# Layernorm sums moved from VectorE to GpSimd, and the statistics of three groups moved into the group loop

## The chip, the cores and the metric

The kernel runs on one core of one Trainium2 chip. The metric is the device time of one execution, in microseconds (us); less is better. Engines are called by the profile's names: PE (TensorE matmuls), PEld (TensorE weight loads), DVE (VectorE), ACT (ScalarE), POOL (GpSimd) and SP (SyncE, here only DMA issue).

## What is computed

A gated cross-attention layer followed by a gated mixture-of-experts layer, for x of shape 32 x 128 x 128 (32 samples of 128 rows, 128 features), 16 heads and 8 experts:

```python
x = x + tanh(g_xattn[0]) * xattn(ctx, layernorm(x), b, seq_len)     # first half
x = x + tanh(g_ffn[0])   * ffn(layernorm(x), wi, bi, wo, bo, ...)   # second half

# ffn: logits = h @ gate_w.T + gate_b; scores = softmax(logits); the top 2 of 8 experts
# per expert e: inter = h @ wi.T + bi + (h @ lora_A[e].T) @ lora_B[e].T
#               out += gate_e * (relu(inter) @ wo.T + bo)
# layernorm: (x - mean) / sqrt(var + 1e-5)
```

## The kernel before, in words

The first half, attention, goes over 16 pairs of samples (`PAIRS`), in a software pipeline of steps `q`, each with two samples `i` and four chunks `c`. The second half goes over 8 groups of 4 samples (`GROUPS`, 512 rows each). All engines have their instruction order written out by hand, and meet only at semaphores; an engine executes its list in order, so that an instruction behind a waiting one waits too.

**Between the halves.** Steps `q` = 16 to 18 (19 on VectorE) finish the attention of the last pairs and already start groups 0 and 1. At `(q - PAIRS, i, c)` VectorE's list has small blocks for the second half. For each group g the second half first needs:

- `X <- X + attention`, one 128 x 512 sum in SBUF. For groups 0 to 2 GpSimd makes it (`residual`, L630), for groups 3 to 7 VectorE does (L1337, at the head of `stats2_of(g, 0)`). Both count in `s_xadd`.
- `stats2_of(g, k)`: the layernorm statistics, four `bn_stats` (L1344), four `bn_aggr` (L1349) and one `tensor_scalar` that adds epsilon (`veps2`, L1351).
- `rsqrt2(g)` (L635) and `normalise2(g)` (four instructions, L643), both on GpSimd.
- `transpose_x` (PE, L1068), `copy_xT` and `x_high` (ACT, L825, L831), `x_low` (GpSimd, L648).

Before, the statistics of groups 3 and 4 come at (1, 0, 3) and (1, 1, 1), of group 5 at (2, 0, 3), of group 6 at (2, 1, 1), and of group 7 in group 0 of the loop, between `sum_experts(0, 1)` and `sum_experts(0, 2)`. Other blocks there are `gates_...` (L1375 to L1423, the choice of the two experts, some twenty small instructions per group), `mask_u` (L1432, four instructions), `u_low` (L1446), and `add_attention(15)` (L1321, L1326), which waits for the last transpose of the attention output on PE (L1055).

**The loop over groups.** PE runs `first_expert(g, c)` (three matmuls of x_part, three of u_part, L1102), `second_expert(g, c)` (three matmuls, L1102), and at the end `out_weights(g)` (32 matmuls, L1137). ACT makes `h1` (L849) after each `first_expert`. VectorE makes `sum_experts(g, c)`, written `hsum` (L1440), after each `second_expert`. The chunks use three PSUM banks in turn, so `first_expert` of chunk number i waits for `s_hs >= i - 2`: `first_expert(g, 3)` cannot start before `sum_experts(g, 0)` has ended. `out_weights(g)` waits for all four sums of its group. VectorE's order in the end of group g is: `sum_experts(g, 3)`, `u_low(g + 1)`, the gates of group g + 2 up to `gates_pick(0)`, `finish(g)` (L1456, four instructions, waits for `out_weights(g)`), the rest of those gates, then in the next group `mask_u(g + 2)` and `sum_experts(g + 1, 0)`. GpSimd's order in a group is `x_low(g + 1)`, `make_base(g)` (L657, L661), `rsqrt2(g + 4)`, `normalise2(g + 4)`.

The functions that the change touches, with what calls them:

Of the kernel before, what the change touches and what calls it, by code (L numbers as in the profile page):

```python
# [18 lines left out]
ALU = mybir.AluOpType  # L19
# [20 lines left out]
def flamingo(nc, x, ctx, seq_len, g_xattn, g_ffn, b, wi, bi, wo, bo, lora_a, lora_b, gate_w, gate_b, out):  # L40
    B, S, D = x.shape
# [12 lines left out]
    GT = 4  # L54
    GROUPS = B // GT
# [7 lines left out]
    with es:  # L63
# [439 lines left out]
        def _(pool):  # L503
# [183 lines left out]
            for q in range(PAIRS + 3):  # L687
                if 0 <= q - 1 < PAIRS:
                    split_max(q - 1)
                if q == 1:  # L690
                    third_part(3)
                if q + 4 < PAIRS:
                    permute_k(q + 4)
                if q >= 2 and q % 2 == 0 and q // 2 + 3 < len(BATCHES):
                    power(q // 2 + 3)
                if q == 2:
                    place_v(0)
                if 2 <= q and 2 * q - 3 < B:
                    place_v(2 * q - 3)
                if q + 4 < PAIRS:  # L700
                    normalise(q + 4)
                if 2 <= q and 2 * q - 2 < B:
                    place_v(2 * q - 2)
                if q == PAIRS - 4:
                    residual(0)
                    residual(1)
                if 1 <= q and q + 3 < PAIRS:
                    third_part(q + 3)

                if q == PAIRS - 3:  # L710
                    rsqrt2(0)
                    normalise2(0)
                if q == PAIRS - 2:
                    weight_low(wiT, wi_part, 2)
                    rsqrt2(1)
                    residual(2)
                if q == PAIRS - 1:
                    normalise2(1)
                    weight_low(bT, b_part, 5)
                if q == PAIRS:  # L720
                    x_low(0)
                    rsqrt2(2)
                    normalise2(2)
                if q == PAIRS + 1:
                    rsqrt2(3)
                    normalise2(3)


            for g in range(GROUPS):
                if g + 1 < GROUPS:  # L730
                    x_low(g + 1)
                make_base(g)
                if g + 4 < GROUPS:
                    rsqrt2(g + 4)
                    normalise2(g + 4)
# [478 lines left out]
        def _(dve):  # L1214
# [117 lines left out]
            def stats2_of(g, k):  # L1332

                o = NST2 * g
                if k == 0 and g >= 3:
                    dve.wait_ge(s_norm, NNORM * 2 * (g + 1))
                    dve.tensor_tensor(X[:, GT * g:GT * (g + 1), :], X[:, GT * g:GT * (g + 1), :],  # L1337
                                      KV[:, GT * g:GT * (g + 1), 0:D], ALU.add).then_inc(s_xadd, 1)
                if k == 0:
                    dve.wait_ge(s_xadd, g + 1)  # L1340
                if k < 2:
                    for t in range(2 * k, 2 * k + 2):
                        n = GT * g + t
                        dve.bn_stats(stats2[:, n, :], X[:, n, :]).then_inc(s_stat2, 1)  # L1344
                else:
                    for t in range(GT):
                        n = GT * g + t
                        dve.wait_ge(s_stat2, o + t + 1)
                        dve.bn_aggr(mv2[:, n, :], stats2[:, n, :]).then_inc(s_stat2, 1)  # L1349
                    dve.wait_ge(s_stat2, o + 2 * GT)  # L1350
                    dve.tensor_scalar(veps2[:, GT * g:GT * (g + 1)], mv2[:, GT * g:GT * (g + 1), 1], EPS, None,  # L1351
                                      ALU.add).then_inc(s_stat2, 1)
# [108 lines left out]
            for q in range(PAIRS + 4):  # L1461
                for i in range(2):
                    m, n = 2 * q + i, 2 * q + i - LAG
                    for c in range(CH):
                        if 0 <= m < B:
                            row_max(m, c)
                        if (q, i, c) == (0, 0, 1):
                            first_rest(2)
                        if (i, c) == ((1, 1) if q == 0 else (0, 3)) and q + 3 < PAIRS:
                            first_rest(q + 3)  # L1470
                        if (i, c) in ((0, 0), (0, 1)) and 0 <= q - 4 < PAIRS and q != PAIRS + 1:
                            add_attention(q - 4, c)
                        later = 12 + c if q == 1 else 12 + 2 * q + c // 2
                        if q >= 1 and i == 1 and later < B and (q == 1 or c % 2 == 1):
                            stats_of(later)
                        if q >= 2 and q % 2 == 0 and (i, c) == (0, 0) and q // 2 + 3 < len(BATCHES):
                            for later in range(*BATCHES[q // 2 + 3]):
                                aggregate(later)
                            variances(q // 2 + 3)

                        for g in range(3):
                            if (q - g, i, c) in ((PAIRS - 4, 1, 1), (PAIRS - 4, 1, 3), (PAIRS - 3, 0, 3)):
                                stats2_of(g, c // 2 if i else 2)
                        at = (q - PAIRS, i, c)
                        if at == (0, 0, 3):
                            gates_shift(0)
                        if at == (0, 1, 1):
                            gates_score(0)
                            gates_top(0)
                        if at == (0, 1, 2):  # L1490
                            gates_pick(0)
                            gates_drop()
                            gates_top(1)
                        if at == (0, 1, 3):
                            add_attention(PAIRS - 3, 0)
                            add_attention(PAIRS - 3, 1)
                            gates_pick(1)
                            gates_end(0)
                        if at == (1, 0, 1):
                            mask_u(0)  # L1500
                        if at == (1, 0, 3):
                            for k in range(3):
                                stats2_of(3, k)
                        if at == (1, 1, 1):
                            for k in range(3):
                                stats2_of(4, k)
                        if at == (2, 0, 2):
                            u_low(0)
                            gates_shift(1)
                        if at == (2, 0, 3):  # L1510
                            for k in range(3):
                                stats2_of(5, k)
                        if at == (2, 1, 0):
                            gates_score(1)
                            gates_top(0)
                            gates_pick(0)
                            gates_drop()
                            gates_top(1)
                            gates_pick(1)
                            gates_end(1)  # L1520
                        if at == (2, 1, 1):
                            for k in range(3):
                                stats2_of(6, k)
                        if (q, i, c) == (PAIRS - 2, 0, 3):

                            dve.wait_ge(s_wr, 16 * 5)
                            dve.tensor_scalar(nbi_col[:, :], bi_col[:, :], -1.0, None, ALU.mult).then_inc(s_shift, 1)
                            dve.tensor_copy(bi_wide[:, :, :],
                                            bi_col[:, :, None].to_broadcast([128, FC, 128])).then_inc(s_shift, 1)
                        if (q, i, c) == (PAIRS - 1, 0, 0):  # L1530
                            dve.wait_ge(s_wT, 4)
                            dve.wait_ge(s_wTc, 6)
                            dve.scalar_tensor_tensor(out=shift[:, :], in0=bo_rows[:, :], scalar=2.0, in1=qk_t[:, 256:256 + D],
                                                     op0=ALU.mult, op1=ALU.add).then_inc(s_shift, 1)


            for g in range(GROUPS):
# [3 lines left out]
                if g == 0:  # L1541
                    mask_u(1)
                sum_experts(g, 1)
                if g == 0:
                    for k in range(3):
                        stats2_of(GROUPS - 1, k)
                sum_experts(g, 2)
                sum_experts(g, 3)
                if g + 1 < GROUPS:
# [8 lines left out]
                if g + 2 < GROUPS:  # L1558
                    gates_drop()
                    gates_top(1)  # L1560
                    gates_pick(1)
                    gates_end(g + 2)


# [22 lines left out]
```

## Time and profile before

| | |
|---|---|
| median of 3 executions | 279.3 us (278.44 to 279.52) |
| the profiled execution's own time | 278.2 us |
| its span in the trace | 276.4 us |
| granted PE clock | full speed throughout |

The profiled execution's time is 1.8 us over its span: what lies around the traced instructions. All rows come from this one execution. A timeline row gives start and length in us from the span's start, engine, line, operation, output and inputs, and how many instructions are merged in it; square brackets give the idle time of the engine before it and what ended that. Merged rows overlap their neighbours by some hundredths of a us, because instructions are pipelined.

### The profile page before, as it was taken

To read this page: it belongs to the slowest core of one execution; us is meant where nothing else is said; L and a number is where in the kernel's file an instruction comes from. 1 tells how busy PE (TensorE), PEld (TensorE's weight loads), DVE (VectorE), ACT (ScalarE), POOL (GpSimd) and SP (SyncE) were. 2 spreads that over 40 slices of the span, in tenths; PEclk is the share of its full clock that TensorE was granted. 3 is DMA by queue.
4 is the path that set the end of the run, shared out by engine and by line. 5 is a ranking of instruction groups with operands and counts; after the bars stand their busy time and mean duration, and the time that the engine had idled before them with its cause. 6 is when DMAs were issued, how large, how long until landed. Compare 5 with 4: busy or idle time off the path is not lost.

```text
span 276.4 us, 8038 instructions
## 1 busy us (share of the span) xinstructions
PE 245.5 (89%) x2966; PEld 184.3 (67%) x2966; DVE 214.0 (77%) x623; ACT 163.0 (59%) x319; POOL 158.5 (57%) x306
## 2 busy tenths in 40 slices
PE   0368979899998999989999979999999999999895
PEld 0135556566665566656567658888888989897865
DVE  4778786899999999997949999858585858585432
ACT  5778785889897989896877642333334242323220
POOL 6888676687877786686892447090919250505120
PEclk9999999999999999999999999999999999999999
DMA  4749997736776866640000000101010101001011
GB/s 110 202 124 209 208 222 181 206 83 196 178 215 160 215 160 162 149 71 6 8 6 2 4 0 0 39 2 38 0 40 0 42 0 30 10 7 31 2 38 38
DMA packets 48461, 23.46 MB, mean 85 GB/s; under 512 B 7680, under 2 KB 48296, under 8 KB 48424
## 3 DMA queue, kind: packets, MB, share of 16 engines
q1 hardware_dynamic: 47520, 22.77, 34.5%
q8 instruction: 24, 0.39, 0.6%
q10 hardware_dynamic: 904, 0.19, 0.4%
q14 instruction: 13, 0.11, 0.1%
HBM read 7.29 MB, written 2.10 MB: 34 GB/s over the span
## 4 chain that ended last, share of the span: by engine, by line
PE 57%; DVE 24%; POOL 5%; ACT 5%; issue 5%; DMA 2%; ACTq 1%; POOLq 0%
PE bank L1102 21%; DVE negmax L1313 11%; PE bank_max L1137 10%; PE bank L1012 7%; PE bank L1044 5%; PE bank L1079 2%; DVE rest L1264 2%; PE bank L1055 2%; PE bank L1095 2%; PE bank L1018 2%; DMA b_rows<-in_L_xattn_b_dram 2%; DVE hsum L1440 2%; ACT stack L760 2%; DVE KV L1326 1%; PE bank L1068 1%
## 5 line engine op out<-in xcount | busy, mean ns | idle before, releaser
L1313 DVE TENSOR_REDUCE negmax<-bank 128x4 f32<-128x512 f32 x128 | 83.3, 680 | 10.7 <-PE bank L1012 10.6
L809 ACT ACTIVATE probs<-bank 128x512 f32<-128x512 f32 x128 | 71.7, 602 | 15.0 <-PE bank L1018 13.9
L1012 PE MATMUL bank<-stack 64*128 64x128 bf16 x512 | 51.9, 235 | 9.6 <-DVE negmax L1313 6.0
L1012 PEld LDWEIGHTS bank<-stack 64*128 64x128 bf16 x512 | 31.7, 101 | 31.2 <-DVE negmax L1313 19.8
L1102 PE MATMUL bank<-u_part,b_part 128*128 128x512 f32 x192 | 52.0, 399 | 0.1
L849 ACT ACTIVATE h<-bank,bi_col 128x512 f32<-128x512 f32 x32 | 22.1, 690 | 49.4 <-PE bank L1102 49.4
L1018 PE MATMUL bank<-stack 64*128 64x128 bf16 x512 | 48.5, 223 | 0.3
L1440 DVE SCALAR_TENSOR_TENSOR hsum<-bank,nbi_col,h 128x512 f32<-128x512 f32 x32 | 23.9, 748 | 24.0 <-PE bank L1102 24.0
L648 POOL TENSOR_TENSOR x_part<-KV,x_part 128x512 fp32r<-128x512 f32 x8 | 10.4, 1301 | 55.8 <-ACT x_part L831 55.8
L1044 PE MATMUL bank<-probs,vpad 128*32 128x128 f32 x1024 | 42.1, 283 | 0.0
L1102 PEld LDWEIGHTS bank<-u_part,b_part 128*128 128x128 f32 x192 | 35.5, 189 | 8.3 <-ACT h L849 0.5
L1018 PEld LDWEIGHTS bank<-stack 64*128 64x128 bf16 x512 | 29.3, 96 | 3.3 <-ACT probs L809 2.2
L1044 PEld LDWEIGHTS bank<-probs,vpad 128*32 128x32 f32 x1024 | 24.5, 110 | 9.8 <-issue 6.4
L1102 PE MATMUL bank<-x_part,wi_part 128*128 128x512 f32 x96 | 28.9, 409 | 1.8 <-DVE hsum L1440 1.8
L1137 PE MATMUL bank_max<-woT,hsum 128*128 128x128 f32 x232 | 28.0, 279 | 2.1 <-DVE hsum L1440 2.1
L1137 PEld LDWEIGHTS bank_max<-woT,hsum 128*128 128x128 f32 x232 | 26.5, 192 | 3.8 <-DVE hsum L1440 3.2
L603 POOL TENSOR_TENSOR part<-rest,part 128x512 bf16<-128x512 f32 x14 | 16.2, 1159 | 20.5 <-ACT part L802 20.5
L643 POOL TENSOR_SCALAR KV<-X,mv,rstd 128x128 f32<-128x128 f32 x32 | 25.6, 810 | 0.8
L1102 PEld LDWEIGHTS bank<-x_part,wi_part 128*128 128x128 f32 x96 | 16.9, 189 | 5.5 <-DVE hsum L1440 2.3
L815 ACT ACTIVATE o_rows<-bank 128x256 f32<-128x256 f32 x32 | 12.4, 388 | 7.5 <-PE bank L1044 7.5
L842 ACT ACTIVATE u_part<-bank 128x512 fp32r<-128x512 f32 x15 | 8.2, 595 | 11.5 <-PE bank L1102 11.5
L968 PE MATMUL bank<-ident,kperm 128*128 128x128 f32 x32 | 8.6, 361 | 6.8 <-ACT kperm L781 6.8
(136 smaller groups left out, 407.0 us busy)
## 6 DMA issues: line engine op xcount, KB each, us to landing
stack<-part SPq DMA_DIRECT2D x96, 128.0 KB, 3.0
KV<-in_ctx_dram SPq DMA_DIRECT2D x5, 512.0 KB, 4.1
X<-in_x_dram SPq DMA_DIRECT2D x7, 256.0 KB, 4.3
out_dram<-res SPq DMA_DIRECT2D x7, 256.0 KB, 2.3
KV<-in_ctx_dram SPq DMA_DIRECT2D x5, 256.0 KB, 5.6
stack<-bias_line SPq DMA_DIRECT2D x7, 48.0 KB
stack<-max_rows SPq DMA_DIRECT2D x13, 24.0 KB
X<-in_x_dram SPq DMA_DIRECT2D x2, 128.0 KB, 2.4
```

The source lines that it names most:

```text
L603: pool.tensor_tensor(pair_part(2, p), halves(rest[:, p % 2, :]), pair_part(1, p), ALU.subtract).then_inc(s_t3, 1)
L643: pool.tensor_scalar(spare(g)[:, t, :], X[:, n, :], mv2[:, n, 0:1], rstd2[:, n:n + 1], ALU.subtract, ALU.mult).then_inc(s_xh2, 1)
L809: act.activation(probs[:, i % 4, :], sc2[i % 2][:, :], ACT.Exp).then_inc(s_exp, 1)
L815: act.activation(o_rows[:, n % 4, :], o_acc[:, 256 * (n % 2):256 * (n % 2) + 256], ACT.Copy).then_inc(s_oc, 1)
L849: act.activation(h1[:, c, :], chunk_bank(i)[:, :], ACT.Relu, bias=bi_col[:, c:c + 1]).then_inc(s_h1, 1)
L1012: mm = pe.matmul(sc1[i % 2][:, j * 128:(j + 1) * 128], stack[at, s, h0 + 2 * j, q0:q0 + 128], stack[at, s, h0 + 2 * j, 512 + q0:640 + q0], ...
L1018: mm = pe.matmul(sc2[k % 2][:, j * 128:(j + 1) * 128], stack[at, t, h0 + 2 * j, 512 + q0:640 + q0], stack[at, t, h0 + 2 * j, q0:q0 + 128], ...
L1044: mm = pe.matmul(o_acc[32 * j:32 * j + 32, c0:c0 + 128], v_window(n, UNITS2[c], j), probs[:, i % 4, j * 128:(j + 1) * 128], start=(c % 2 = ...
L1102: mm = pe.matmul(dst, w[a], v[b], start=(start and k == 0), stop=(closed or (stop and k == 2)), skip_group_check=closed)
L1137: mm = pe.matmul(out_bank(g, t)[:, t * 128:(t + 1) * 128], hsum[:, c, t * 128:(t + 1) * 128], woT[:, c, :], start=(c == 0), stop=(c == FC ...
L1313: dve.tensor_reduce(negmax[:, p % 2, n % 2, 8 * (u // 2) + u % 2:8 * (u // 2) + u % 2 + 7:2], bank_cols(sc1[i % 2]), AX.X, ALU.max, negate ...
L1440: dve.scalar_tensor_tensor(out=hsum[:, c, :], in0=chunk_bank(i)[:, :], scalar=nbi_col[:, c:c + 1], in1=h1[:, c, :], op0=ALU.max, op1=ALU.a ...
```

## The change

GpSimd makes the sums of groups 3 to 7 too: `residual(3)` after `x_low(0)`, `residual(4)` at the next step, and `residual(g + 5)` in groups 0 to 2 of the loop, after `make_base(g)`. VectorE loses the sum from `stats2_of`. The statistics of group 4 move from (1, 1, 1) to (2, 0, 3), where those of group 5 stood; those of groups 5, 6 and 7 move to the end of groups 0, 1 and 2 of the loop, behind `gates_end(g + 2)`.

```diff
@@ gpsimd, the steps between the halves
                 if q == PAIRS:
                     x_low(0)
+                    residual(3)
                     rsqrt2(2)
                     normalise2(2)
                 if q == PAIRS + 1:
+                    residual(4)
                     rsqrt2(3)
                     normalise2(3)
@@ gpsimd, the loop over groups
                     x_low(g + 1)
                 make_base(g)
+                if g + 5 < GROUPS:
+                    residual(g + 5)
                 if g + 4 < GROUPS:
@@ vector, stats2_of(g, k)
-                if k == 0 and g >= 3:
-                    dve.wait_ge(s_norm, NNORM * 2 * (g + 1))
-                    dve.tensor_tensor(X[:, GT * g:GT * (g + 1), :], X[:, GT * g:GT * (g + 1), :],
-                                      KV[:, GT * g:GT * (g + 1), 0:D], ALU.add).then_inc(s_xadd, 1)
                 if k == 0:
                     dve.wait_ge(s_xadd, g + 1)
@@ vector, the steps between the halves
                         if at == (1, 0, 3):
                             for k in range(3):
                                 stats2_of(3, k)
-                        if at == (1, 1, 1):
-                            for k in range(3):
-                                stats2_of(4, k)
...
                         if at == (2, 0, 3):
                             for k in range(3):
-                                stats2_of(5, k)
+                                stats2_of(4, k)
...
-                        if at == (2, 1, 1):
-                            for k in range(3):
-                                stats2_of(6, k)
@@ vector, the loop over groups
                 sum_experts(g, 1)
-                if g == 0:
-                    for k in range(3):
-                        stats2_of(GROUPS - 1, k)
                 sum_experts(g, 2)
...
                     gates_end(g + 2)
+                if g + 5 < GROUPS:
+                    for k in range(3):
+                        stats2_of(g + 5, k)
```

## Rows read from the trace of the kernel before

**Rows 1.** The page, part 1: busy time, share of the span, instructions.

```profile
PE 245.5 (89%) x2966; PEld 184.3 (67%) x2966; DVE 214.0 (77%) x623; ACT 163.0 (59%) x319; POOL 158.5 (57%) x306
```


**Rows 2.** Busy us by stretch: stretch, length, PE, PEld, DVE, ACT, POOL; then granted clock.

```profile
152.70:170.64 17.94, 15.49 (x142) 11.60 (x141) 17.06 (x66) 8.73 (x18) 10.55 (x12) 1.00 0.00 1
...
188.82:203.20 14.38, 14.38 (x89) 12.56 (x89) 10.19 (x35) 5.09 (x9) 7.71 (x8) 1.00 0.07 19
```


**Rows 3.** The chain of waits in order of time: start us, length us, piece.

```profile
152.75 0.37 DVE rsum L1321
...
170.64 3.84 PE bank_max L1137 x32
```


**Rows 4.** Timeline of PE, 159 to 189 us: start us, length us, operation.

```profile
159.92 0.38 PE L1055 MATMUL bank<-ident,o_rows 128*128 128x128 f32 x2
...
161.28 0.86 PE L1102 MATMUL bank<-x_part,wi_part 128*128 128x512 f32 x3
...
165.35 0.97 PE L1102 MATMUL bank<-x_part,wi_part 128*128 128x512 f32 x3 [1.83 <-DVE hsum L1440]
166.16 1.54 PE L1102 MATMUL bank<-u_part,b_part 128*128 128x512 f32 x6
...
178.23 0.87 PE L1102 MATMUL bank<-x_part,wi_part 128*128 128x512 f32 x3
...
180.31 0.85 PE L1102 MATMUL bank<-x_part,wi_part 128*128 128x512 f32 x3
181.00 1.56 PE L1102 MATMUL bank<-u_part,b_part 128*128 128x512 f32 x6
...
184.98 3.84 PE L1137 MATMUL bank_max<-woT,hsum 128*128 128x128 f32 x32
```


**Rows 5.** Timeline of DVE from 143 us: start us, length us, operation.

```profile
144.65 0.33 DVE L1411 SCALAR_TENSOR_TENSOR score<-hot,score 128x32 f32<-128x32 f32 x1
...
155.35 0.68 DVE L1337 TENSOR_TENSOR X<-X,KV 128x512 f32<-128x512 f32 x1
156.07 0.87 DVE L1344 BATCH_NORM_STATS2 stats<-X 128x6 f32<-128x128 f32 x4
...
157.34 0.18 DVE L1386 TENSOR_REDUCE lsum<-lexp 128x4 f32<-128x32 f32 x1
...
160.77 0.68 DVE L1337 TENSOR_TENSOR X<-X,KV 128x512 f32<-128x512 f32 x1
...
162.67 1.19 DVE L1351 TENSOR_SCALAR veps<-mv 128x4 f32<-128x4 f32 x1
163.78 0.34 DVE L1321 RECIPROCAL rsum<-bank 128x32 f32<-128x32 f32 x1
...
167.19 0.69 DVE L1337 TENSOR_TENSOR X<-X,KV 128x512 f32<-128x512 f32 x1
...
169.18 1.41 DVE L1440 SCALAR_TENSOR_TENSOR hsum<-bank,nbi_col,h 128x512 f32<-128x512 f32 x2
...
177.41 0.76 DVE L1432 TENSOR_TENSOR u<-bank,hot 128x256 f32<-128x256 f32 x2
...
178.74 0.74 DVE L1440 SCALAR_TENSOR_TENSOR hsum<-bank,nbi_col,h 128x512 f32<-128x512 f32 x1
```


**Rows 6.** Instructions of line L1351: engine, operation, count, ns least/median/most.

```profile
L1351 DVE TENSOR_SCALAR veps<-mv x8: 170/174/1189, 118.2 to 169.1; 128x4 f32<-128x4 f32 x8
```


**Rows 7.** Timeline of POOL, 139 to 180 us: start us, length us, operation.

```profile
142.09 3.19 POOL L643 TENSOR_SCALAR KV<-X,mv,rstd 128x128 f32<-128x128 f32 x4
...
150.72 1.39 POOL L635 TENSOR_TENSOR rstd<-veps,half_neg 128x4 f32<-128x4 f32 x1 [5.03 <-DVE veps L1351]
...
162.55 1.29 POOL L648 TENSOR_TENSOR x_part<-KV,x_part 128x512 fp32r<-128x512 f32 x1 [7.20 <-ACT x_part L831]
...
179.03 1.30 POOL L648 TENSOR_TENSOR x_part<-KV,x_part 128x512 fp32r<-128x512 f32 x1 [8.15 <-ACT x_part L831]
```


**Rows 8.** Instructions of line L630: engine, operation, count, ns least/median/most.

```profile
L630 POOL TENSOR_TENSOR X<-X,KV x3: 1266/1282/1286, 110.0 to 127.6; 128x512 f32<-128x512 f32 x3
```


## The prediction

> **What bounds the kernel now.** I read the page first. PE is busy for 89% of the span, VectorE for 77% [rows 1]. Those are averages over two halves, so the second view is the busy time by stretch. In a group of the loop PE is busy for all 14.38 of 14.38 us and VectorE for 10.19 [rows 2]: the loop runs at PE's pace. From 152.70 to 170.64 us, where the attention runs out and group 0 begins, it is the other way round: VectorE 17.06 of 17.94 us, PE 15.49 [rows 2]. The third view, the chain of waits, says the same in another way: from 152.75 us it lies on VectorE, and goes back to PE only with `out_weights(0)` at 170.64 us [rows 3]. So VectorE's list sets the time in these 18 us, and what it costs is seen on PE's own timeline: `first_expert(0, 3)` starts at 165.35 us after PE idled 1.83 us for `hsum` [rows 4], and `out_weights(0)` starts late as well.
>
> How much can come back is read by setting group 0 against group 1, which has the same PE list. From the start of `first_expert(g, 2)` to the end of `out_weights(g)` group 1 takes (184.98 + 3.84) - 178.23 = 10.59 us [rows 4]. Group 0 takes from 161.28 [rows 4] to 170.64 + 3.84 = 174.48 us [rows 3], 13.20 us. The difference, 2.61 us, is all that VectorE costs PE here. 1.99 us of it is the wait ahead of `first_expert(0, 3)` (165.35 - 161.28 against 180.31 - 178.23 [rows 4]), and 0.62 us is the rest, mainly the wait ahead of `out_weights(0)`.
>
> **What the change removes between the halves.** Ahead of 152.75 us the statistics of group 4 and the sum of group 3 go; VectorE was free for the attention's last pairs there when PE's transpose came, so this alone gives nothing. After 152.75 us three things go from the list [rows 5]. At (2, 0, 3) statistics of group 4 without a sum stand for those of group 5 with one: 156.07 - 155.35 = 0.72 us less. At (2, 1, 1) all of group 6 goes: 163.78 - 160.77 = 3.01 us. In group 0 all of group 7 goes: 169.18 - 167.19 = 1.99 us. Together 5.72 us of VectorE's chain, more than twice what PE can take back.
>
> Is the first wait then gone in full? `hsum(0, 0)` released PE at 165.35 us [rows 4]. Without 0.72 + 3.01 us VectorE's list would reach that point at 161.6 us; it then waits for other things, `add_attention(15)` for the transpose of 159.92 + 0.38 us [rows 4] and `hsum` for `second_expert(0, 0)`, which ends where `first_expert(0, 2)` starts, 161.28 us. So it ends near 161.3 + 0.74 [rows 5] plus a hand-over, 162.2 us at most, and PE needs it at 161.28 + 2.08 = 163.36 us. More than 1 us is to spare. `mask_u(1)` follows (1.33 us, 178.74 - 177.41 [rows 5]) and ends before the transposes that need it. From there the sums follow PE as in group 1. I take the whole 2.61 us; the lower bound is 2.0 us, if only the first wait goes.
>
> **What it adds on GpSimd.** One `residual` takes 1.28 us [rows 8]. `residual(3)` and `rsqrt2(2)`, `normalise2(2)` behind it run in a stretch where GpSimd then idles: `rsqrt2(3)` waits 5.03 us, until 150.72 us, for VectorE's statistics [rows 7]. Two sums are 2.56 us, half of that. The new waits of `stats2_of(3)` and `stats2_of(4)` on VectorE for GpSimd are therefore met: `residual(3)` is done at about 142.3 us, and the statistics stand at about 148.6; `residual(4)` comes behind `normalise2(2)` and the last copies of v, at about 148.3 us, and is wanted at 155.35 us. If it were late, the gates of group 1 and all else in VectorE's list would stand behind it; the cover is 7 us. In the loop GpSimd is busy 7.71 of 14.38 us [rows 2] and idles 8.15 us ahead of `x_low` of a group [rows 7]. A `residual` more makes it 9.0 us. What is late next is `normalise2(g + 4)` by 1.28 us, which PE wants more than a group later. Cost nothing.
>
> **What it adds on VectorE in the loop.** The statistics without the sum take 157.34 - 156.07 = 1.27 us [rows 5]. They stand behind `gates_end` and ahead of `mask_u(g + 2)` and `hsum(g + 1, 0)`, and for the latter PE's `first_expert(g + 1, 3)` waits. On average VectorE has 4 us to spare per group, but not here. `hsum(1, 0)` ended at 178.74 + 0.74 = 179.48 us [rows 5], and `first_expert(1, 3)` started at 180.31 us [rows 4]: 0.83 us of cover. Part of the 1.27 us takes the place of a short hand-over ahead of `mask_u`; I take 1.15 to 1.27, so 1.2 us. With 0.05 us from a sum's end to PE's start (169.18 + 1.41 = 170.59 us [rows 5] and 170.64 [rows 3]), PE is late by 1.2 + 0.05 - 0.83 = 0.42 us. A late start also costs a little more, because the weight load is no longer under the matmul ahead: three x_part matmuls took 166.16 - 165.35 = 0.81 us behind the wait and 181.00 - 180.31 = 0.69 us without [rows 4], 0.12 us more. So 0.54 us a group. PE is full in these groups [rows 2], so nothing takes it back, and `finish(g)` of the next group moves with PE: the stall comes in groups 1, 2 and 3. Bounds for one: 0.37 us (1.15, no load) and 0.66 us (1.27, the load, 0.05 for a stretched gate). Three are 1.6 us, 1.1 to 2.0.
>
> The gates' small instructions may be stretched where `normalise2` now lies under them for 1.28 us more. At 142.09 to 145.28 us the two already overlap [rows 7], and the worst gate instruction took 0.33 us [rows 5]. I take 0.05 us a group for it, inside the bounds above. In the Trainium skill, "SBUF — State Buffer", section "Who interferes with whom", a VectorE instruction with two SBUF inputs contends with a GpSimd one that reads SBUF, and the later of the two blocks fully. By row the cost is the 0.05 us a group; by that rule it is a rival, below. This trace does not show such a full block for the gates.
>
> **Sum.** -2.6 + 1.6 = -1.0 us. The profiled execution's 278.2 us would be 277.2; it lay 1.1 us under the median of 279.3, which would be 278.3 us, 0.4% less. The bounds are -1.5 (2.6 and 1.1) and 0.0 (2.0 and 2.0), so 277.8 to 279.3 us. A change of 0.5%, 1.4 us, is about what a measurement of this kernel can tell from none.
>
> **Rivals.** *The statistics in the loop are hidden.* If VectorE's place behind `gates_end` had room for them, only the gain would be left: 279.3 - 2.6 = 276.7 us. For it speaks the spare 4 us per group; against it the 0.83 us at the one place. Chance 0.14.
>
> *The epsilon instruction meets `x_low` (slower).* `veps2` normally takes 0.17 us, but once 1.19 [rows 6]: at 162.67 us, just after `x_low` had started on GpSimd at 162.55 us, and it ended as that did [rows 5, 7]. In the loop the new one comes about 1.1 us behind the place where `mask_u` stood, 177.41 us, so at 178.5, and `x_low` starts at 179.03 us [rows 7]: it is ahead by 0.5 us. The point from which it decides: if VectorE is later by more than 0.5 us, it waits to 179.03 + 1.30 = 180.33 us, `mask_u` and `hsum` end at 182.40, and PE stalls 2.26 us a group in place of 0.54. Three groups: 279.3 - 2.6 + 6.8 = 283.5 us. Chance 0.07. The same section of the Trainium skill says that `tensor_scalar` in a two-port mode and GpSimd exclude each other for a whole instruction; by that rule, the trace agrees (1.19 against 0.17 us).
>
> *The gates are blocked by `normalise2`.* Each of its four instructions takes 3.19 / 4 = 0.80 us [rows 7], and the shift of 1.28 us puts at most two more under the gates. If these blocked a gate instruction in full, `finish` would be late by up to 1.6 us less the small slack; at one block a group, 0.8 us, the sum is 278.3 + 2.4 = 280.7 us. Against it stands the 0.33 us. Chance 0.08.
>
> *PE does not get its time back in group 0,* because behind VectorE something else is late, such as ScalarE's part of group 0 or the hand-overs. Then 0 to 1.6 us of gain stand against 1.6 us of stalls: 279.3 to 280.9 us. For it speaks that so many lists meet here; against it the 1 us to spare. Chance 0.13. My forecast has 0.58.
>
> **How the numbers follow.** Predicted is 278.3 us. The range leaves out the collision, most of the blocked gates and the top of the last case: 276.6 to 280.4 us; the likeliest case's own is 277.8 to 279.3. Faster by over 0.5% (under 277.9 us) are the hidden statistics and a quarter of the forecast's: 0.30. Slower by over 0.5% (over 280.7) are the collision, half of the blocked gates, some of the last case and a little for the measurement: 0.16. The rest is 0.54.
>
> **What would show it.** In the changed profile: PE without idle time ahead of `first_expert(0, 3)` and `out_weights(0)`, the latter ending 13.20 - 2.61 = 10.6 us behind the start of `first_expert(0, 2)`; L1337 gone and L630 eight times; PE idle (or its weight load) released by `hsum` once in each of groups 1, 2 and 3, by about half a us, so that these groups take 14.9 us and group 4 14.4 us; `veps2` always near 0.17 us. The prediction is wrong if a group with statistics takes 14.4 us or over 15.5 us, or if group 0 keeps a wait.

## The result, and the profile after

| | before | changed |
|---|---|---|
| median of 20 executions | 278.38 us | 276.29 us |
| the profiled execution's span | 276.4 us | 274.0 us |

The ratio is 0.9931, with a 95% interval of 0.9912 to 0.9949: 1.9 us less, 1.4 to 2.4. It leaves out disturbed executions, such as one of 1162.61 us of the kernel before. The forecast was 1.0 us less, 278.3 us, in a range of 276.6 to 280.4. The changed kernel is 2.0 us under the forecast time and 0.3 us under the range.

The first view of the changed kernel is the busy time by stretch: stretch, its length, then the busy us of PE, PEld, DVE, ACT and POOL with the number of instructions, and the granted clock. The stretches are the end of group 0 (from the start of `first_expert(0, 2)`) and groups 1 to 4, each up to the end of its `out_weights`.

```profile
160.26:170.83 10.57, 10.57 (x71) 9.49 (x70) 7.63 (x21) 3.89 (x8) 8.96 (x9) 1.00 0.00 0
170.83:185.64 14.81, 14.63 (x90) 12.49 (x89) 11.32 (x45) 5.08 (x9) 8.97 (x9) 1.00 0.07 19
185.64:200.43 14.79, 14.62 (x89) 12.48 (x89) 11.22 (x44) 5.08 (x9) 8.96 (x9) 1.00 0.07 19
200.43:215.23 14.80, 14.58 (x89) 12.47 (x89) 11.20 (x44) 5.08 (x9) 7.73 (x8) 1.00 0.06 18
215.23:229.57 14.34, 14.34 (x89) 12.56 (x89) 10.16 (x35) 5.08 (x9) 3.61 (x3) 1.00 0.07 20
```

The end of group 0 takes 10.57 us where it took 13.20 [rows 3, 4]: 2.63 us less, and PE is never idle in it. Groups 1, 2 and 3 take 14.81, 14.79 and 14.80 us where a group took 14.38 [rows 2]; group 4, with no statistics at its head, takes 14.34. The timeline of PE (start, length, operation, idle time before and its releaser) shows where:

```profile
160.26 0.86 PE L1106 MATMUL bank<-x_part,wi_part 128*128 128x512 f32 x3
...
162.34 0.87 PE L1106 MATMUL bank<-x_part,wi_part 128*128 128x512 f32 x3
...
166.99 3.84 PE L1141 MATMUL bank_max<-woT,hsum 128*128 128x128 f32 x32
...
174.60 0.85 PE L1106 MATMUL bank<-x_part,wi_part 128*128 128x512 f32 x3
...
177.03 0.95 PE L1106 MATMUL bank<-x_part,wi_part 128*128 128x512 f32 x3 [0.18 <-DVE hsum L1440]
...
181.80 3.84 PE L1141 MATMUL bank_max<-woT,hsum 128*128 128x128 f32 x32
```

`first_expert(0, 3)` follows at 162.34 us with no wait and `out_weights(0)` at 166.99 us with none. In the kernel before PE idled 1.83 us ahead of the first [rows 4] and 0.43 us ahead of the second:

```profile
170.64 3.84 PE L1137 MATMUL bank_max<-woT,hsum 128*128 128x128 f32 x32 [0.43 <-DVE hsum L1440]
```

In group 1 `first_expert(1, 3)` starts 177.03 - 174.60 = 2.43 us behind `first_expert(1, 2)` where it was 2.08 [rows 4]: it now waits for `hsum(1, 0)`. The timeline of DVE shows what stands ahead of that sum, `bn_stats` from 173.64 us, the epsilon instruction (`bn_aggr` lies between them) and `mask_u(2)`:

```profile
145.59 1.43 DVE L1417 TENSOR_TENSOR lsum<-top 128x4 f32<-128x4 f32 x1
...
160.46 0.75 DVE L1440 SCALAR_TENSOR_TENSOR hsum<-bank,nbi_col,h 128x512 f32<-128x512 f32 x1 [0.27 <-PE bank L1106]
...
173.64 0.86 DVE L1344 BATCH_NORM_STATS2 stats<-X 128x6 f32<-128x128 f32 x4
...
174.82 0.17 DVE L1351 TENSOR_SCALAR veps<-mv 128x4 f32<-128x4 f32 x1
174.90 0.76 DVE L1432 TENSOR_TENSOR u<-bank,hot 128x256 f32<-128x256 f32 x2
...
176.23 1.40 DVE L1440 SCALAR_TENSOR_TENSOR hsum<-bank,nbi_col,h 128x512 f32<-128x512 f32 x2
```

and the timeline of POOL has the sums, and `x_low` of groups 0, 1 and 2:

```profile
138.62 1.27 POOL L648 TENSOR_TENSOR x_part<-KV,x_part 128x512 fp32r<-128x512 f32 x1
139.85 1.27 POOL L630 TENSOR_TENSOR X<-X,KV 128x512 f32<-128x512 f32 x1
...
145.74 1.27 POOL L630 TENSOR_TENSOR X<-X,KV 128x512 f32<-128x512 f32 x1
...
161.53 1.30 POOL L648 TENSOR_TENSOR x_part<-KV,x_part 128x512 fp32r<-128x512 f32 x1 [7.08 <-ACT x_part L835]
...
165.16 1.28 POOL L630 TENSOR_TENSOR X<-X,KV 128x512 f32<-128x512 f32 x1
...
175.40 1.31 POOL L648 TENSOR_TENSOR x_part<-KV,x_part 128x512 fp32r<-128x512 f32 x1 [4.72 <-ACT x_part L835]
```

The epsilon instruction starts at 174.82 us, takes 0.17 us and has ended 0.4 us before `x_low(2)` starts at 175.40 us. One line was not foreseen: at 145.59 us DVE needs 1.43 us for an addition of 128 x 4 numbers (L1417) that otherwise takes 0.15 us. It ends at 147.02 us, as `residual(4)` does, whose start is recorded at 145.74 us.

From `first_expert(0, 2)` to the end of the span 276.4 - 161.28 = 115.12 us in the trace before [rows 4] became 274.0 - 160.26 = 113.74 us, 1.4 us less. The other 1.0 us of the spans' difference was there already when `first_expert(0, 2)` began, and at `x_low(0)`, 138.62 us here, 139.70 before: ahead of the first instruction that the change touches.

### The profile page after: what moved, and what is told of

Its sections match the earlier page's. It is cut to its first block, busy times and chain, and to the rows that moved or that the text cites. A ratio compares the mean times of both kernels' runs of the same rounds, so it can differ in the third digit from the quotient of the medians.

```text
span 274.0 us, 8038 instructions
## 1 busy us (share of the span) xinstructions
PE 245.4 (90%) x2966; PEld 184.0 (67%) x2966; DVE 211.0 (77%) x618; ACT 163.0 (59%) x319; POOL 163.7 (60%) x311
## 4 chain that ended last, share of the span: by engine, by line
PE 54%; DVE 26%; ACT 5%; POOL 5%; issue 5%; DMA 2%; ACTq 1%; POOLq 0%; DVEq 0%
PE bank L1106 19%; DVE negmax L1317 12%; PE bank_max L1141 9%; PE bank L1016 6%; PE bank L1048 6%; DVE rest L1268 3%; PE bank L1083 3%; PE bank L1099 2%; PE bank L1059 2%; PE bank L1022 2%; DMA b_rows<-in_L_xattn_b_dram 2%; DVE hsum L1440 2%; DVE u L1432 2%; ACT stack L764 2%; ACT probs L813 1%
```

## The experiments

Each median is that of the kernel's own executions; a ratio is against the kernel before on the same chip.

### Sums to GpSimd alone, in one row

```diff
@@ gpsimd: residual(3) after x_low(0), as in the changed kernel
                 if q == PAIRS + 1:
+                    residual(4)
+                    residual(5)
+                    residual(6)
                     rsqrt2(3)
                     normalise2(3)
+                    residual(7)
@@ stats2_of: no sum on VectorE; all statistics stay where they were before
```

> The five sums go to GpSimd, the statistics of groups 3 to 7 stay where they were in the kernel before. My theory (VectorE's list bounds the kernel only from 152.7 to 170.6 us, PE can take back 2.6 us there, and statistics at the ends of groups 0 to 2 cost a stall of 0.4 us each): VectorE loses three sums of 0.72 us ahead of hsum(0, 3), and its epsilon instruction of group 6 no longer meets x_low(1), so another 1.0 us; hsum(0, 0) ends about 2.4 us earlier, in time for PE. The full 2.6 us come back and no stall is paid: 2.6 us under the kernel before, about 1.2 us under the changed one. Rival (the move of the statistics is what brings the gain): only 1.4 us under the kernel before, slower than the changed one.

The median of its 6 executions is 280.87 us, beside 278.59 for the kernel before; 2.6 us less were expected, so this is a miss. No ratio is given: five of the six had a granted clock under 1, down to 0.976, and the one at full clock took 276.70 us, where the kernel before at full clock has a median of 278.0. The times alone thus do not say how this kernel compares; the trace says what went wrong in it. The first two fences are its timelines of DVE and POOL, the third that of PE.

```profile
146.34 3.89 DVE L1418 TENSOR_TENSOR lsum<-top 128x4 f32<-128x4 f32 x1
```

```profile
146.49 3.72 POOL L630 TENSOR_TENSOR X<-X,KV 128x512 f32<-128x512 f32 x3
```

```profile
151.44 0.66 PE L1100 MATMUL bank<-ident,u 128*128 128x128 f32 x4 [2.21 <-DVE u L1433]
...
153.69 2.06 PE L1084 MATMUL bank<-agT,KV 128*128 128x136 f32 x8
```

L1418 here is L1417 of the other kernels. VectorE's addition of 128 x 4 numbers, two inputs in SBUF, stands for 3.89 us and ends at 150.23, as the third of three GpSimd sums in a row does (146.49 + 3.72 = 150.21 us). `mask_u(0)` is late, PE idles 2.21 us for it, and eight matmuls that take 1.19 us in the changed kernel take 2.06 us behind the gap, where the granted clock is 0.76 from 150 to 154 us and 0.81 from 154 to 158. From `x_low(0)` to `first_expert(0, 2)` it is 165.00 - 139.38 = 25.62 us, 4.0 us more than the 21.64 of the changed kernel. So GpSimd's sums can hold VectorE, and PE's idle time has a second price. Behind that the trace has what the theory said, 171.74 + 3.84 - 165.00 = 10.58 us for the end of group 0 and 14.38 us for each of groups 1 to 3. But VectorE had 4 us more to catch up here, so this is a weak test of the theory's place.

### The moves alone, sums on VectorE

```diff
@@ the changed kernel, with the sum back in stats2_of
+                if k == 0 and g >= 3:
+                    dve.wait_ge(s_norm, NNORM * 2 * (g + 1))
+                    dve.tensor_tensor(X[...], X[...], KV[...], ALU.add).then_inc(s_xadd, 1)
@@ gpsimd: no residual(3) to residual(7)
```

> The statistics move as in the changed kernel, the sums stay on VectorE (groups 3 to 7). My theory: the 2.6 us of group 0 come back all the same, but each of the three statistics in the loop is 0.72 us longer, so each stall is 0.43 + 0.72 = 1.15 us, and the epsilon instruction, 0.7 us later, now starts just behind x_low on GpSimd and is held until that ends, about 1.1 us more. With the hold 2.6 - 6.8, so 4.1 us over the kernel before; without it 0.9 us over it. Rival (the loop hides VectorE's work): about 2 us under it.

Median 282.4 us, ratio 1.0141 (1.0099 to 1.0184): 3.9 us slower, beside 4.1 expected with the hold. Timelines of DVE, POOL and PE:

```profile
176.56 1.20 DVE L1351 TENSOR_SCALAR veps<-mv 128x4 f32<-128x4 f32 x1
```

```profile
176.43 1.31 POOL L648 TENSOR_TENSOR x_part<-KV,x_part 128x512 fp32r<-128x512 f32 x1 [5.95 <-ACT x_part L831]
```

```profile
168.02 3.84 PE L1137 MATMUL bank_max<-woT,hsum 128*128 128x128 f32 x32
...
179.79 0.97 PE L1102 MATMUL bank<-x_part,wi_part 128*128 128x512 f32 x3 [1.92 <-DVE hsum L1440]
...
184.56 3.84 PE L1137 MATMUL bank_max<-woT,hsum 128*128 128x128 f32 x32
```

`x_low(2)` starts at 176.43 us, the epsilon instruction at 176.56, 0.13 us too late: it takes 1.20 us and ends at 177.76, as `x_low(2)` does (177.74). PE idles 1.92 us, the period from `out_weights` to `out_weights` is 184.56 - 168.02 = 16.54 us, 2.16 over 14.38. Groups 2 and 3 have the same hold (1.19 and 1.16 us) and the same wait. So the gap of 0.4 us in the changed kernel exists only because the sums left VectorE: these moves of the statistics pay only together with the sums. Behind the second of the three waits, of 1.92 us again, the granted clock was 0.50 from 198 to 200 us, and that period took 18.11 us instead of 16.54; behind the first and the third it stayed full.

### Statistics one block later

```diff
@@ the changed kernel, vector, the loop over groups
                 sum_experts(g, 0)
                 if g == 0:
                     mask_u(1)
+                if 1 <= g <= 3:
+                    for k in range(3):
+                        stats2_of(g + 4, k)
                 sum_experts(g, 1)
...
                     gates_end(g + 2)
-                if g + 5 < GROUPS:
-                    for k in range(3):
-                        stats2_of(g + 5, k)
```

> The changed kernel with the statistics of groups 5, 6 and 7 one block later: behind mask_u and sum_experts(g + 1, 0) and ahead of sum_experts(g + 1, 1), in groups 1 to 3, for which PE has time. My theory: the three stalls of 0.43 us vanish, 1.3 us under the changed kernel, 2.6 to 3 us under the kernel before; groups 1 to 3 take 14.4 us. Rival (a statistics block costs PE wherever it stands in the loop): the same as the changed kernel.

Median 274.83 us, ratio 0.9881 (0.9844 to 0.9919): 3.3 us under the kernel before, the lowest median of all. Timelines of PE and DVE:

```profile
166.67 3.84 PE L1141 MATMUL bank_max<-woT,hsum 128*128 128x128 f32 x32
...
174.27 0.85 PE L1106 MATMUL bank<-x_part,wi_part 128*128 128x512 f32 x3
...
176.36 0.87 PE L1106 MATMUL bank<-x_part,wi_part 128*128 128x512 f32 x3
...
181.05 3.84 PE L1141 MATMUL bank_max<-woT,hsum 128*128 128x128 f32 x32
```

```profile
174.78 0.74 DVE L1440 SCALAR_TENSOR_TENSOR hsum<-bank,nbi_col,h 128x512 f32<-128x512 f32 x1
175.44 0.86 DVE L1344 BATCH_NORM_STATS2 stats<-X 128x6 f32<-128x128 f32 x4
...
176.61 0.79 DVE L1351 TENSOR_SCALAR veps<-mv 128x4 f32<-128x4 f32 x1
177.32 0.74 DVE L1440 SCALAR_TENSOR_TENSOR hsum<-bank,nbi_col,h 128x512 f32<-128x512 f32 x1
```

The period is 181.05 - 166.67 = 14.38 us and `first_expert(1, 3)` starts 2.09 us behind `first_expert(1, 2)`: the stall is gone. Here the epsilon instruction takes 0.79 us, under an addition of `make_base` on GpSimd (L657, 176.33 to 177.37 us), and `hsum(1, 1)` is late. It costs PE nothing: that sum is needed first by `out_weights(1)`, at 181.05 us.

### The kernel before again, and PE kept busy in its wait

> The kernel before, unchanged, as a control for the 1.1 us by which the profiled execution of the changed kernel was ahead before the first edited instruction. If that is spread from execution to execution, the ratio is 1.000 and the step in which x_low(0) starts differs from 139.70 us by up to a us in this trace too. If the changed kernel's first part is faster by its code, this one starts x_low(0) at 139.7 us and those of the other kernels of this call start it near 138.6 us.

Median 278.57 us, ratio 0.9995 (0.9968 to 1.0021). Its `x_low(0)` started at 139.59 us. That alone does not decide, since it is within 0.1 us of the first trace. But in the eleven traces of this document, whose instruction lists are the same up to that point, it started between 137.96 us (the statistics made longer) and 140.74 us (`residual(4)` later), and in the two traces of the changed kernel at 138.62 and 140.38 us. So the 1.0 us by which the changed kernel's profiled execution was ahead is spread between executions.

The control showed more. The fences show PE behind its wait in the timeline, and the stretch from 166 to 170 us in the view by stretch:

```profile
161.16 0.86 PE L1102 MATMUL bank<-x_part,wi_part 128*128 128x512 f32 x3
...
165.25 0.97 PE L1102 MATMUL bank<-x_part,wi_part 128*128 128x512 f32 x3 [1.84 <-DVE hsum L1440]
166.06 2.27 PE L1102 MATMUL bank<-u_part,b_part 128*128 128x512 f32 x6
...
171.62 3.84 PE L1137 MATMUL bank_max<-woT,hsum 128*128 128x128 f32 x32
```

```profile
166.00:170.00 4.00, 4.00 (x16) 3.37 (x16) 3.75 (x14) 0.69 (x1) 3.90 (x6) 0.58 0.00 0
```

The wait of 1.84 us is the same as in the profile before, but the six matmuls behind it take 2.27 us instead of 1.54 [rows 4], and the granted clock from 166 to 170 us is 0.58 (1.00 in the profile before), PE thus at its lower level (1.2 GHz) for most of it. From `first_expert(0, 2)` to the end of `out_weights(0)` it is 14.30 us here, 13.20 in the profile before: 1.1 us. Over the whole span this is a clock of 0.994. The kernel before shows it in 6 of the 17 executions that ran beside this control (median 278.88 us, against 278.0 for the 11 at full clock), the control itself shows 0.994 or less in 5 of 12, the changed kernel in 1 of 20. To test whether the wait is the cause, four matmuls were put into it:

```diff
@@ the kernel before, tensor, group 0
                 second_expert(g, 1)
+                if g == 0:
+                    pe.wait_ge(s_xTc, 3)
+                    for _ in range(4):
+                        pe.matmul(qk_t[:, 0:128], woT[:, 0, :], woT[:, 1, :], start=True, stop=True)
                 first_expert(g, 3)
```

> The kernel before with four matmuls more on PE (128 x 128 by 128, into a PSUM bank that is free then), in the wait ahead of first_expert(0, 3); they fill about 1.1 of its 1.83 us and are thrown away, the output stays the reference's. Theory (about a third of the executions of the kernel before show 0.994 as granted clock, because PE's wait there is followed by a stretch at half clock, which costs these executions 0.9 us; the change takes the wait away and so wins 0.4 us on average beside the 1.4 us of its own): executions under 1.0 become rare, the median falls by 0.3 to 0.5 us, ratio 0.998 to 0.999. Rival (the lower clock has nothing to do with this wait): a third of the executions still show 0.994 and the ratio is 1.000 or more.

```profile
163.01 1.05 PE L1206 MATMUL bank<-woT 128*128 128x128 f32 x8
165.03 0.97 PE L1102 MATMUL bank<-x_part,wi_part 128*128 128x512 f32 x3 [0.96 <-DVE hsum L1444]
```

The profile counts two matmuls for each of the four. PE's idle time is 0.96 us, and `first_expert(0, 3)` is no earlier: 4.09 us behind `first_expert(0, 2)`, where it was 4.07. None of 12 executions was under full clock, 6 of 17 of the kernel before beside them were (279.13 us against 277.67). The medians are 277.84 and 278.21 us, the ratio 0.9978 (0.9951 to 1.0006). The counts speak for the theory, as does the place of the dip, directly behind a wait of 1.84 to 2.21 us, in all three traces with a clock of 0.994 (the control, the sums in one row, the moves alone). The 0.4 us is as expected, but its interval reaches to no change.

### Sums alone, apart

```diff
@@ the first experiment, gpsimd
                 if q == PAIRS + 1:
                     residual(4)
+                    rsqrt2(3)
                     residual(5)
                     residual(6)
-                    rsqrt2(3)
                     normalise2(3)
                     residual(7)
```

> As the first kernel (sums to GpSimd, statistics unmoved), but with the sums of groups 5 and 6 behind rsqrt2(3) and not in one row behind that of group 4. Theory (in the first kernel VectorE's small sum of the gates was held for 3.9 us by three GpSimd sums in a row, and PE then ran at a lower clock): the hold shrinks to the 1.4 us of one sum, PE does not wait for mask_u, the full 2.6 us of group 0 come back and no stall is paid in groups 1 to 3; 3 us under the kernel before, about 1.3 us under the changed one, the same as with the statistics behind hsum. Rival (the statistics must leave the stretch between the halves for the gain to come): 1.4 us or less under the kernel before.

Median 277.03 us, ratio 0.9940 (0.9912 to 0.9968): 1.7 us under the kernel before, half of what was expected, and the same as the changed kernel beside it (277.11 us, below), where 1.3 us less were expected. The fences are the timelines of PE, DVE and POOL.

```profile
162.26 0.97 PE L1107 MATMUL bank<-x_part,wi_part 128*128 128x512 f32 x3 [0.16 <-DVE hsum L1441]
...
167.93 3.84 PE L1142 MATMUL bank_max<-woT,hsum 128*128 128x128 f32 x32 [0.82 <-DVE hsum L1441]
```

```profile
150.81 1.29 DVE L1352 TENSOR_SCALAR veps<-mv 128x4 f32<-128x4 f32 x1
...
165.29 1.28 DVE L1352 TENSOR_SCALAR veps<-mv 128x4 f32<-128x4 f32 x1
```

```profile
150.80 2.50 POOL L630 TENSOR_TENSOR X<-X,KV 128x512 f32<-128x512 f32 x2
...
165.26 1.28 POOL L661 TENSOR_TENSOR base<-base,X 128x512 f32<-128x512 f32 x1
```

PE waits again, 0.16 us and 0.82 us, and the end of group 0 takes 167.93 + 3.84 - 159.86 = 11.91 us, 1.34 more than in the changed kernel. Twice an epsilon instruction (L1352 here) begins within some hundredths of a us of a GpSimd addition and is held for it: at 150.81 and at 165.29 us, 1.29 and 1.28 us. Both stand in a list of VectorE without idle time, so each delays what follows by 1.1 us; the expectation had left them out. Groups 1 to 3 have no stall (14.38 us). So the sums alone, apart, bring as much as the whole change: what the holds cost there the stalls cost here.

### The hold taken away, and the statistics made longer

The first of two runs is the kernel with the statistics one block later, and `residual(4)` behind `rsqrt2(3)` instead of ahead of it:

> The kernel with the statistics behind hsum, and residual(4) behind rsqrt2(3). Theory: the gates' last sum (L1417) of group 0 takes 0.15 us again in place of 1.4, but PE has its own work until mask_u is needed, so the time stays the same within 0.2 us. Rival (the 1.4 us hold is on the path): 1 us faster.

```profile
147.71 0.19 DVE L1417 TENSOR_TENSOR lsum<-top 128x4 f32<-128x4 f32 x1
```

L1417 takes 0.19 us again. Median 275.51 us, ratio 0.9875 (0.9832 to 0.9918), beside 0.9881 without this edit: the same, but the intervals are too wide to exclude 1 us. The traces do: from `x_low(0)` to `first_expert(0, 2)` it is 162.32 - 140.74 = 21.58 us here, and 159.94 - 138.31 = 21.63 us with the hold. The 1.3 us hold of the changed kernel is off the path.

The second is the changed kernel with another set of `bn_stats`, into a spare tile, behind each of the three statistics in the loop:

```diff
                 if g + 5 < GROUPS:
                     for k in range(3):
                         stats2_of(g + 5, k)
+                    for t in range(GT):
+                        dve.bn_stats(again[:, t, :], X[:, GT * (g + 5) + t, :])
```

> The changed kernel, with four more bn_stats to a spare tile behind each of the three statistics in the loop (0.8 us more on VectorE, behind the epsilon instruction, which thus does not meet x_low). The output stays the reference's. Theory: PE's stalls go from 0.43 to 1.2 us, so 3 x 0.8 = 2.4 us over the changed kernel, and no epsilon instruction is held. Rival (VectorE has hidden room there): under 1 us more.

```profile
166.35 3.84 PE L1142 MATMUL bank_max<-woT,hsum 128*128 128x128 f32 x32
...
177.14 0.96 PE L1107 MATMUL bank<-x_part,wi_part 128*128 128x512 f32 x3 [0.93 <-DVE hsum L1441]
...
181.93 3.84 PE L1142 MATMUL bank_max<-woT,hsum 128*128 128x128 f32 x32
...
197.49 3.84 PE L1142 MATMUL bank_max<-woT,hsum 128*128 128x128 f32 x32
```

The periods are 15.58 and 15.56 us, 0.77 over the changed kernel's 14.80; the four `bn_stats` had put `mask_u(2)` back by 0.78 us, so every us more at this place is paid in full. Median 279.03 us, ratio 1.0015 (0.9987 to 1.0043), 1.9 us over the changed kernel beside it; 3 x 0.77 = 2.3 us were due, and the 0.4 us between them is within the two intervals.

The changed kernel ran once more beside them:

> The changed kernel once more, beside the others on one chip: 0.993 of the kernel before, and the clock at full speed in nearly all executions, where the kernel before shows 0.994 in about a third.

Median 277.11 us, ratio 0.9951 (0.992 to 0.9982), a little nearer to 1 than the first measurement, with which its interval overlaps. 1 of 12 executions was at 0.994 or less, 12 of 27 of the kernel before beside it. Its trace repeats the first: the end of group 0 takes 10.57 us, groups 1 to 3 take 14.80 to 14.83, group 4 takes 14.38.

## What of the prediction held, and why its time was too high

**VectorE's list bounds the kernel only between the halves, and PE can take back 2.61 us there.** Right for the stretch itself at full clock: 2.63 us, both waits gone, `hsum(0, 0)` at 160.46 to 161.21 us, 1.1 us ahead of `first_expert(0, 3)`.

**GpSimd has room for the sums, at no cost.** Right in the time, not in the reason, and so by luck. The new waits of `stats2_of` cost PE nothing. But `residual(4)` held VectorE's list for 1.3 us, at an instruction that I had not looked at. `mask_u(0)` ended at 148.83 us by its rows, and PE's transposes of its second half began at 148.90: the hold used up the cover to 0.1 us. Two sums more in a row cost 2.21 us of PE's time, and the clock behind it. With the sums apart it was two epsilon instructions that met GpSimd's additions.

**Three statistics in the loop cost one stall each.** Right in place, number and cause; the size was a little over: 0.41 to 0.43 us measured, 0.54 in the sum (bounds 0.37 and 0.66). Three are 1.3 us, not 1.6. In group 1 the block put VectorE back by 1.13 us instead of 1.2 (`mask_u` starts 174.90 - 173.51 = 1.39 us behind the gates' last instruction, 177.41 - 177.15 = 0.26 before), `first_expert(1, 3)` came 0.35 us later instead of 0.42, and its late start cost 0.10 us instead of 0.12. Statistics one block later, and the longer ones, show the mechanism from both sides.

**The sum, -1.0 us, is the step that failed,** and in it the sentence that 2.61 us "is all that VectorE costs PE here". It counted PE's wait of 1.83 us [rows 4] by its length and put its effect on the clock at nothing. The runs show that behind this wait the clock falls in about four of ten executions (24 of 61 that ran beside the experiments). It cost 1.1 us in the one trace that shows it, and the medians of the two kinds differ by 0.9 to 1.5 us; that is some 0.4 us on average, an estimate. The profile shown before was one of the other kind, with a full clock throughout; the row of the wait was there, its second price was not. The second term is the stalls, 0.3 us too large: from `first_expert(0, 2)` on the traces show -1.4 us instead of -1.0.

The third is not a step of the reasoning but the starting point: 279.3 us was the median of three executions, that of 20 is 278.38, 0.9 us less. It is the largest part of the 2.0 us by which the time was missed, and without it the time would lie in the range; but the change itself, -1.9 us, is still nearly twice the forecast's. With all three, 278.38 - 1.4 - 0.4 = 276.6 us, against 276.29. The 0.3 us left are within the interval of the ratio. The split into 1.4 and 0.4 us comes from traces and counts, and the medians do not confirm it: in the set of the second run of the changed kernel, its 11 executions at a clock of 0.999 or more have a median of 277.07 us and the 15 of the kernel before at full clock 277.73, 0.7 us apart and not 1.4. The executions of one kernel at full clock spread by over 2 us there, so how much each part gives stays open within some tenths of a us.

**The rivals.** *Hidden in the loop*: excluded by the stalls. *PE does not get its time back in group 0*: excluded, it got 2.63 us. *The epsilon instruction meets `x_low`*: it did not in the changed kernel, with 0.4 us to spare, and did, with the price as reckoned, where the sum stayed ahead of it (2.16 us a group against 2.26). *The gates blocked by `normalise2`*: it did not happen, the longest gate instruction under `normalise2` took 0.38 us. The section "Who interferes with whom" of "SBUF — State Buffer" in the Trainium skill has two SBUF inputs on VectorE contend with GpSimd's reads of SBUF; the traces agree when GpSimd makes a `tensor_tensor` of two inputs (1.43 and 3.89 us against 0.15) and do not show it as a full block when GpSimd makes the `tensor_scalar` of `normalise2` (0.80 us each; 0.41 us at most for a gate instruction in any trace).

## What to carry to other kernels

Average room on an engine says nothing about a place in its list: the same 1.27 us of statistics cost 0.43 us a group ahead of `hsum(g, 0)`, and nothing behind it. When work moves to GpSimd, lay its new large additions under VectorE's timeline and look for epsilon-like `tensor_scalar`s and for additions from SBUF that would start under them or just ahead of them. One such addition was harmless here, three in a row were not, and two epsilon instructions in VectorE's full list cost half of the gain. A long wait of PE can cost more than its length, and one profile may not show it: compare the granted clock over many executions.

## What the runs showed of the hardware that was not expected

- A `tensor_tensor` on VectorE of 128 x 4 numbers with both inputs in SBUF (L1417), recorded as starting 0.15 us ahead of a GpSimd `tensor_tensor` of 128 x 512, ended only with it: 0.15 us became 1.43. With three GpSimd additions in a row it became 3.89 us, so it did not get between them. These are cases of one place in the list.
- The epsilon instruction, a `tensor_scalar` of 128 x 4 with one tensor input, was held to the end of a GpSimd `tensor_tensor` that had started up to 0.29 us before (0.77 to 1.29 us instead of 0.17). Behind the first of two GpSimd additions in a row it did get between them (150.81 to 152.10 us, the sums apart). Once it started in the same hundredth of a us as the addition, 169.63 us with the sums in one row, and was not held (0.17 us).
- Under GpSimd's `tensor_scalar` with one input tensor of 128 x 128 (0.80 us) VectorE's two-input instructions of 128 x 32 mostly took their 0.19 us, and 0.41 us at most (statistics one block later).
- Behind a wait of PE of 1.84 us the granted clock was 0.58 over 4 us in one trace, and full behind one of 1.83 us in another of the same kernel. Over the whole execution it was under 1 in 24 of 61 of the kernel before, and with 0.96 us of wait in 0 of 12.
